# Layer 0 aggregation of a GAT kernel: the weighted rows go to fourteen places of their own, and a gather waits for the multiplication that read its place instead of for the sums

## The chip, the cores and the metric

One Trainium2 chip, one of its cores. The metric is the device time of one execution in microseconds (us). The kernel before was run three times, with a median of 2488.86 us.

## What is computed

A graph attention network of two layers, followed by a mixture-of-experts feed-forward part, on 3125 nodes with 768 features and 50000 edges sorted by destination. The part that matters here is the first layer's message passing, with 8 heads of 96 features:

```python
h = (x @ W1).reshape(n, 8, 96)
e = leaky_relu(al_s[src] + al_d[dst], 0.2)
ex = exp(e - segment_max(e, dst)[dst])
alpha = ex / (segment_sum(ex, dst)[dst] + 1e-16)
out = segment_sum(h[src] * alpha[:, :, None], dst)      # per edge: fetch a row, weight it by head, add it to its node
```

The second layer is the same with one head, and the experts come after it.

## The kernel before

**Stages.** One program calls a row of functions one after the other: the set-up, the features h of all nodes (written to a table `feat_tab` in memory), the attention scores, `aggregate` (this is the changed one), the next layer's features, its scores, `aggregate_rows`, the routing and the experts. Each function is a block with one hand-written instruction stream for each engine, and the streams meet by semaphores alone. On one engine the instructions run in the order in which they are written.

**The work of `aggregate`.** The edges are cut into NT = 392 tiles of 128 edges. For each tile:

1. POOL (GpSimd, L1449) issues one indirect DMA, called a gather here, that fetches 128 rows of 776 floats from `feat_tab` (768 features and 8 columns for the denominator), 397 KB in all, into one of RING = UN = 14 places. Place k = t mod 14 of tile t is `rows[k]`: places 0 to 6 lie in the buffer `ring`, 7 to 10 in `work`, 11 in `wg`, 12 and 13 in `edges`. So a trace row tells by its buffer which places it is about.
2. DVE (VectorE, L1479) multiplies the row by its 8 edge weights, which lie in PSUM (`ex_ps`), **in place**: it reads `rows[k]` and writes `rows[k]`.
3. PE (TensorE, L1502) adds the tile to the sums of a window of 64 destination nodes in PSUM: two matmuls with the tile's 128x64 one-hot matrix, one for each half of 388 columns. The profile shows four matmul records for these two. Where a window of 64 nodes ends inside a tile, the next window is opened by two more matmuls (`opened`, 49 in all).

Beside this, DVE builds the one-hot matrices for 7 tiles at a time (`hots`, L1462) and copies 14 tiles' weights to PSUM (`weights`, L1470). ACT (ScalarE) copies each finished window out of PSUM (L1582, two instructions), prepares the one-hot matrix of the next opening (L1570) and stores the sums of 128 nodes at a time (L1587).

**What orders the work.** The loop of DVE, per turn i of 14 tiles and half j: `hots(i, j)`, in the second half `weights(i + 1)`, then seven multiplications. The waits are:

- the gather of tile t (from t = 14 on) waits until PE has finished the sums of tile t - 13: `tile_mm >= t - UN + 2`, at L1448;
- the multiplication waits for its gather's data (`row_in[k]`), L1477;
- PE's sums wait for the multiplication (`msg_ready`) and, at each seventh tile, for the one-hot matrices (`hot_ready`), L1510 and L1511;
- `hots(i, j)` waits until PE has started the previous batch of seven (`batch_mm >= i * 2 + j`), L1461, since two batches of one-hot matrices are kept;
- ACT's copy of a window waits until PE has opened the next (`open_mm`), L1580, and an opening waits until ACT has emptied the bank (`flushed`).

`big` is a large buffer that holds features in other stages. Nothing in this stage uses it.

Of the kernel before, what the change touches and what calls it, by code (L numbers as in the profile page):

```python
# [4 lines left out]
P = 128  # L5
# [7 lines left out]
UN = 14  # L13
# [34 lines left out]
ROW = 776  # L48
HALF = ROW // 2
HC = ROW // 8  # L50
# [57 lines left out]
def gnn_ffn(nc, io, out):  # L108
    with ExitStack() as ctx:
# [34 lines left out]
        big = sb("big", [P, KC * NP])  # L144
# [1282 lines left out]
        def aggregate():  # L1427
            H = HEADS[0]
            L = "_a0"
            row_in = [sem(f"row_in{k}" + L) for k in range(RING)]  # L1430
            msg_ready, hot_ready, open_ready, tile_mm, open_mm, table_ready = (
                sem(n + L) for n in ("msg", "hot_ready", "open_hot", "tile_mm", "open_mm", "open_table"))
# [3 lines left out]
            ex_ps = [mps[:, h, 0:UN * H].rearrange("p (t h) -> p t h", h=H) for h in range(2)]  # L1436
            iota_ps = tps[:, 1, 0:WIN]
            rows = msg_rows + [edges[:, j * ROW:(j + 1) * ROW] for j in range(RING - len(msg_rows))]
            hot_x = hot_open.rearrange("p (b n) -> p b n", b=NW)

            with nc.Block() as block:
                @block.gpsimd
                def _(pool):
                    nc.gpsimd.memset(zeros, 0.0).then_inc(zero_set, 1)
                    for t in range(NT):
                        k = t % UN
                        if t >= UN:
                            pool.wait_ge(tile_mm, t - UN + 2)  # L1448
                        pool.indirect_dma_start(rows[k], None, feat_tab[0],  # L1449
                                                bass.IndirectOffsetOnAxis(ap=src_t[:, t:t + 1], axis=0)).then_inc(row_in[k], 16)  # L1450

                @block.vector
                def _(dve):
                    V = nc.vector
                    near = iota_ps.unsqueeze(1)

                    def hots(i, j):

                        first = i * UN + j * BATCH
                        if i > 0:  # L1460
                            dve.wait_ge(batch_mm, i * 2 + j)  # L1461
                        V.tensor_tensor(onehot[:, j * BATCH:(j + 1) * BATCH, :], near.to_broadcast([P, BATCH, WIN]),  # L1462
                                        dst_rel[:, first:first + BATCH].unsqueeze(2).to_broadcast([P, BATCH, WIN]),
                                        ALU.is_equal).then_inc(hot_ready, 1)

                    def weights(i):

                        if i >= 2:
                            dve.wait_ge(msg_ready, (i - 1) * UN)
                        V.tensor_copy(ex_ps[i % 2], ex[:, i * UN:(i + 1) * UN, :]).then_inc(ex_set, 1)  # L1470

                    def messages(i, j):

                        if j == 0:
                            dve.wait_ge(ex_set, i + 2)
                        for k in range(j * BATCH, (j + 1) * BATCH):
                            dve.wait_ge(row_in[k], i * 16 + 16)  # L1477
                            r3 = rows[k].rearrange("p (h c) -> p h c", h=H)
                            V.tensor_tensor(r3, r3, ex_ps[i % 2][:, k, :].unsqueeze(2).to_broadcast([P, H, HC]),  # L1479
                                            ALU.mult).then_inc(msg_ready, 1)  # L1480
                    V.tensor_copy(iota_ps, iota_f[:, 0:WIN]).then_inc(ex_set, 1)
                    dve.wait_ge(ex_set, 1)
                    hots(0, 0)
                    hots(0, 1)
                    weights(0)
                    V.tensor_tensor(hot_x, near.to_broadcast([P, NW, WIN]),
                                    dst_open[:, :].unsqueeze(2).to_broadcast([P, NW, WIN]), ALU.is_equal).then_inc(table_ready, 1)
                    for i in range(TURNS):
                        for j in range(2):
                            if i > 0:  # L1490
                                hots(i, j)
                            if j == 1 and i < TURNS - 1:
                                weights(i + 1)
                            messages(i, j)

                @block.tensor
                def _(pe):
                    def sums(hot, k, bank, start):

                        row = rows[k]  # L1500
                        for c in range(WPB):
                            m = nc.tensor.matmul(acc[c * WIN:(c + 1) * WIN, bank, 0:HALF], hot, row[:, c * HALF:(c + 1) * HALF],  # L1502
                                                 start=start, stop=True, skip_group_check=True)
                            if c == 0 and not start and k % BATCH == 0:
                                m.then_inc(batch_mm, 1)
                        return m

                    def added(i, k, bank):
                        if k % BATCH == 0:
                            pe.wait_ge(hot_ready, i * 2 + (k // BATCH + 1))  # L1510
                        pe.wait_ge(msg_ready, i * UN + (k + 1))  # L1511
                        sums(onehot[:, k, :], k, bank, False).then_inc(tile_mm, 1)

                    def opened(b, k, bank):
                        pe.wait_ge(open_ready, b)
                        pe.wait_ge(flushed, b)
                        sums(next_x[bank], k, bank, True).then_inc(open_mm, 1)
                    pe.wait_ge(zero_set, 1)
                    for c in range(WPB):
                        m = nc.tensor.matmul(acc[c * WIN:(c + 1) * WIN, 0, 0:HALF], zeros[:, 0:WIN], zeros[:, 0:HALF], start=True, stop=True,  # L1520
                                             skip_group_check=True)
                    m.then_inc(open_mm, 1)
                    bits_reg = [pe.alloc_register("bits0")]
                    regs = [pe.alloc_register(f"open0_{j}") for j in range(3)]
                    bank_reg = pe.alloc_register("bank0")
                    pe.reg_mov(bank_reg, 0)

                    def single(i, k, b0, b1):
                        bank = pe.snap(bank_reg, min_val=0, max_val=1)
                        with pe.If(bank > 0):  # L1530
                            added(i, k, 1)
                        with pe.Else():
                            added(i, k, 0)
                        with pe.If(b1 > b0):
                            with pe.Fori(b0 + 1, b1 + 1) as b:
                                pe.reg_mov(bank_reg, b & 1)
                                bank = pe.snap(bank_reg, min_val=0, max_val=1)
                                with pe.If(bank > 0):
                                    opened(b, k, 1)
                                with pe.Else():  # L1540
                                    opened(b, k, 0)

                    with pe.Fori(0, TURNS) as i:
                        pe.load(bits_reg, open_bits[0:1, ds(i, 1)])
                        bits = pe.snap(bits_reg[0], min_val=0, max_val=(1 << UN) - 1)
                        for k in range(0, UN, 2):
                            with pe.If((bits & (3 << k)) > 0):
                                pe.load(regs, pair_ends[0:1, ds(i * (UN * 4) + k * 4, 3)])
                                b0, b1, b2 = [pe.snap(r, min_val=0, max_val=NW - 1) for r in regs]
                                single(i, k, b0, b1)  # L1550
                                single(i, k + 1, b1, b2)
                            with pe.Else():
                                bank = pe.snap(bank_reg, min_val=0, max_val=1)
                                with pe.If(bank > 0):
                                    added(i, k, 1)
                                    added(i, k + 1, 1)
                                with pe.Else():
                                    added(i, k, 0)
                                    added(i, k + 1, 0)
                    nc.tensor.matmul(tps[0:32, 0, 0:1], iota_f[:, 0:32], iota_f[:, 0:1], start=True, stop=True,  # L1560
                                     skip_group_check=True).then_inc(open_mm, 1)
# [756 lines left out]
```

## Time and profile before

| | us |
|---|---|
| runs of the kernel before | 2483.84, 2488.86, 2489.7 (median 2488.86) |
| the profiled execution, its own time | 2504.38 |
| its span in the profile | 2502.5 |
| mean granted clock of TensorE | 0.899 of full |
| the stage from the first gather of L1449 to the end of its last copy | about 529 to 1111 |

One execution was profiled; every duration below comes from it. A time in a timeline row is counted from the start of the span. The "idle before" of a row is the time its engine did nothing just ahead of it, with what the profile takes to have ended that. Where an instruction waits for several things, or the named one is long done, the profile's releaser isn't the real one; the text says so where that matters. A row with xN joins N instructions that ran on without a gap.

### The profile page before, as it was taken

Reading aid. Unit: us, or ns where it says so; the run is one execution under the profiler, and the core shown is the slowest. Engines: PE = TensorE matmul, PEld = TensorE weight load, DVE = VectorE, ACT = ScalarE, POOL = GpSimd, SP = SyncE. Lnnn points to the kernel's source line nnn. Section 1 sums busy time; section 2 is a strip of 40 time slices with the busy share of each in tenths; the row PEclk is TensorE's granted clock in tenths of the full one; section 3 lists DMA queues with packets and bytes.
Section 4 is the critical chain, followed back from the end, with each engine's and each line's share of the span. In section 5 each row is a group of like instructions: output and inputs, shape, how many; then the busy total and the mean of one; then the engine's idle time right before and its main releaser. Section 6 shows DMA issues by size and latency. Waiting matters only on the chain. (4 is left out here: it accounts for less than half of the span.)

```text
span 2502.5 us, 32295 instructions
## 1 busy us (share of the span) xinstructions
PE 1881.4 (75%) x8856; PEld 1001.4 (40%) x8857; DVE 1312.2 (52%) x2900; ACT 715.7 (29%) x1721; POOL 1263.7 (50%) x1279
## 2 busy tenths in 40 slices
PE   1837887957777777756789867778777775899997
PEld 1325555522222222224445433333323323677775
DVE  7626667847676667658467412344343447522221
ACT  1514433211001101017223233443444440133332
POOL 5065553036666666632321135666666660277775
PEclk9968998979988999988889978888999996799999
DMA  5322321168888888889589597898998986388886
GB/s 177 114 59 56 100 62 43 54 201 288 289 285 291 287 285 292 281 274 277 154 220 265 124 295 268 314 319 305 316 311 310 323 306 235 84 139 139 138 138 104
DMA packets 171459, 533.04 MB, mean 213 GB/s; under 512 B 35105, under 2 KB 66060, under 8 KB 171122
## 3 DMA queue, kind: packets, MB, share of 16 engines
q0 software_dynamic: 99088, 379.24, 53.5%
q1 hardware_dynamic: 61490, 123.21, 14.1%
q10 hardware_dynamic: 10800, 29.70, 3.0%
q8 instruction: 28, 0.46, 0.1%
q14 instruction: 53, 0.43, 0.0%
HBM read 444.94 MB, written 87.10 MB: 213 GB/s over the span
## 5 line engine op out<-in xcount | busy, mean ns | idle before, releaser
L1502 PE MATMUL acc<-ring,work 128*64 128x388 f32 x880 | 208.2, 556 | 85.2 <-issue 61.3
L1796 PE MATMUL acc<-ring,work 128*64 128x384 f32 (+1 forms) x880 | 203.6, 570 | 80.4 <-issue 72.1
L920 PE MATMUL acc<-wg,work 128*128 128x384 f32 x600 | 224.7, 517 | 26.9 <-issue 17.7
L1640 POOL DMA_INDIRECT ring<-feat_tab,src_t x196 | 187.3, 955 | 109.4 <-PE acc L1796 46.6
L1907 ACT ACTIVATE work<-big,edges 128x64 f32<-128x64 f32 x392 | 135.9, 427 | 352.0 <-DMA edges<-in_w_slow 190.3
L1449 POOL DMA_INDIRECT ring<-feat_tab,src_t x196 | 185.3, 945 | 98.1 <-issue 47.6
L1253 PE MATMUL acc<-wg,work 128*128 128x384 f32 x600 | 217.8, 511 | 8.1 <-issue 6.3
L2109 POOL DMA_INDIRECT out_rows<-ring,wg x114 | 178.0, 1562 | 81.2 <-ACT ring L2206 60.0
L1754 DVE COPY work<-acc 64x384 f32<-64x384 f32 x100 | 56.0, 560 | 308.3 <-DMA edges<-in_w_scale 261.6
L1479 DVE TENSOR_TENSOR ring<-ring,mps 128x776 f32<-128x776 f32 x196 | 183.5, 959 | 56.9 <-DMA ring<-feat_tab,src_t 48.1
L869 POOL DMA_INDIRECT edges<-score_tab,src_p x152 | 147.4, 970 | 116.1 <-issue 45.2
L1582 ACT ACTIVATE work<-acc 64x388 f32<-64x388 f32 x100 | 48.8, 488 | 518.2 <-DMA edges<-in_a_dst 492.2
L1502 PE MATMUL acc<-work 128*64 128x388 f32 x504 | 124.4, 552 | 51.6 <-issue 40.7
L1502 PEld LDWEIGHTS acc<-ring,work 128*64 128x64 f32 x880 | 65.4, 148 | 227.1 <-issue 171.6
L1796 PEld LDWEIGHTS acc<-ring,work 128*64 128x64 f32 x880 | 71.7, 153 | 203.3 <-issue 196.0
L920 PEld LDWEIGHTS acc<-wg,work 128*128 128x128 f32 x600 | 114.2, 201 | 96.5 <-issue 41.4
L2243 DVE TENSOR_TENSOR edges<-acc,wg 128x192 f32<-128x192 f32 x57 | 20.4, 358 | 240.6 <-issue 124.7
L1253 PEld LDWEIGHTS acc<-wg,work 128*128 128x128 f32 x600 | 113.6, 197 | 78.1 <-issue 14.6
L1796 PE MATMUL acc<-work 128*64 128x384 f32 (+1 forms) x504 | 111.8, 519 | 41.9 <-issue 38.3
L1640 POOL DMA_INDIRECT work<-feat_tab,src_t x112 | 106.6, 952 | 60.8 <-issue 27.8
L1449 POOL DMA_INDIRECT work<-feat_tab,src_t x112 | 105.8, 945 | 61.3 <-issue 25.0
L2143 PE MATMUL acc<-big,work 128*128 x684 | 123.6, 331 | 12.3 <-issue 11.4
(388 smaller groups left out, 3498.4 us busy)
## 6 DMA issues: line engine op xcount, KB each, us to landing
ring<-lo_rows SPq DMA_DIRECT2D x49, 256.0 KB
edges<-in_w_slow SPq DMA_DIRECT2D x28, 384.0 KB, 6.0
edges<-in_w_hebb POOLq DMA_DIRECT2D x28, 384.0 KB, 7.2
edges<-in_w_fast POOLq DMA_DIRECT2D x28, 384.0 KB, 8.6
unit_sum<-edges SPq DMA_DIRECT2D x28, 384.0 KB, 5.9
out_rows<-work SPq DMA_DIRECT2D x52, 192.0 KB
feat_tab<-work ACTq DMA_DIRECT2D x25, 388.0 KB
agg_raw<-work ACTq DMA_DIRECT2D x25, 388.0 KB
```

Of the source, the lines that this page charges most:

```text
L869: pool.indirect_dma_start(src_s[:, t, :], None, score_tab, bass.IndirectOffsetOnAxis(ap=src_p[:, t:t + 1], axis=0)).then_inc(gather_in, 16)
L920: m = nc.tensor.matmul(acc[:, sl * 2 + c, 0:C // 2], xT[sl][:, k, :], wg[:, k, c * (C // 2):(c + 1) * (C // 2)], start=(k == 0), stop=(k = ...
L1253: m = nc.tensor.matmul(acc[:, sl * 2 + c, 0:C // 2], xT[sl][:, k, :], wg[:, k, c * (C // 2):(c + 1) * (C // 2)], start=(k == 0), stop=(k = ...
L1449: pool.indirect_dma_start(rows[k], None, feat_tab[0], bass.IndirectOffsetOnAxis(ap=src_t[:, t:t + 1], axis=0)).then_inc(row_in[k], 16)
L1479: V.tensor_tensor(r3, r3, ex_ps[i % 2][:, k, :].unsqueeze(2).to_broadcast([P, H, HC]), ALU.mult).then_inc(msg_ready, 1)
L1502: m = nc.tensor.matmul(acc[c * WIN:(c + 1) * WIN, bank, 0:HALF], hot, row[:, c * HALF:(c + 1) * HALF], start=start, stop=True, skip_group_ ...
L1640: pool.indirect_dma_start(rows[k][:, 0:C], None, feat_tab[1], bass.IndirectOffsetOnAxis(ap=src_t[:, t:t + 1], axis=0)).then_inc(row_in[k], 16)
L1754: ins = V.tensor_copy(r[w * WIN:(w + 1) * WIN, c * CHUNK:c * CHUNK + n], acc[c * WIN:(c + 1) * WIN, q % 2, 0:n])
L1796: m = nc.tensor.matmul(acc[c * WIN:(c + 1) * WIN, bank, 0:n], hot, row[:, c * CHUNK:c * CHUNK + n], start=start, stop=True, skip_group_che ...
L1907: ins = nc.scalar.activation(onehot[:, j * BATCH + k, :], gaps[j][:, k, :], ACT.Relu, bias=ex[:, first + k:first + k + 1], scale=neg_ex[:, ...
L2109: pool.indirect_dma_start(out[c], bass.IndirectOffsetOnAxis(ap=slots[:, 2, t:t + 1].bitcast(i32), axis=0), y_rows[t % TU][:, c * (C // 2): ...
L2143: m = nc.tensor.matmul(acc[:, 2, 0:HID], xTs[k][:, c, :], big[:, ds(e * HID + c * EH, HID)], start=(c == 0), stop=(c == KC - 1))
```

## The change

The products get a place of their own: `msgs[k]` is the k-th piece, one row long, of `big`, for k = 0 to 13. The multiplication reads `rows[k]` and writes `msgs[k]`, and PE reads `msgs[k]`. With this the waits change:

- the gather of tile t waits until DVE has multiplied tile t - 14 (`msg_ready >= t - 13`), not until PE has summed tile t - 13;
- the multiplication of tile t (from t = 14 on) waits also until PE has summed tile t - 13 (`tile_mm >= t - 12`), after its wait for the data.

No instruction is added, removed or moved on any engine: POOL, DVE and PE have as many as before, in the same order. The lines move: the gather stands at L1450 and PE's sums at L1505 in the changed kernel.

```diff
@@ -1436,6 +1436,7 @@
             rows = msg_rows + [edges[:, j * ROW:(j + 1) * ROW] for j in range(RING - len(msg_rows))]
+            msgs = [big[:, k * ROW:(k + 1) * ROW] for k in range(UN)]
             hot_x = hot_open.rearrange("p (b n) -> p b n", b=NW)
@@ -1445,7 +1446,7 @@
                     for t in range(NT):
                         k = t % UN
                         if t >= UN:
-                            pool.wait_ge(tile_mm, t - UN + 2)
+                            pool.wait_ge(msg_ready, t - UN + 1)
                         pool.indirect_dma_start(rows[k], None, feat_tab[0],
@@ -1475,8 +1476,10 @@
                             dve.wait_ge(row_in[k], i * 16 + 16)
-                            r3 = rows[k].rearrange("p (h c) -> p h c", h=H)
-                            V.tensor_tensor(r3, r3, ex_ps[i % 2][:, k, :].unsqueeze(2).to_broadcast([P, H, HC]),
+                            if i > 0:
+                                dve.wait_ge(tile_mm, (i - 1) * UN + k + 2)
+                            m3, r3 = (of[k].rearrange("p (h c) -> p h c", h=H) for of in (msgs, rows))
+                            V.tensor_tensor(m3, r3, ex_ps[i % 2][:, k, :].unsqueeze(2).to_broadcast([P, H, HC]),
                                             ALU.mult).then_inc(msg_ready, 1)
@@ -1497,7 +1500,7 @@
                     def sums(hot, k, bank, start):
-                        row = rows[k]
+                        row = msgs[k]
```

## Rows read from the trace of the kernel before

**Rows 1.** Busy us (and count) by engine, TensorE clock, DMA share, GB/s, of the stage.
```profile
527.00:1112.00 585.00, 419.60 (x1770) 129.74 (x1770) 404.32 (x478) 58.73 (x150) 370.91 (x393) 0.92 0.85 283
```

**Rows 2.** The gathers of L1449: durations, first and last start, idle before them.
```profile
L1449 POOL DMA_INDIRECT ring<-feat_tab,src_t x196: 940/946/955, 529.1 to 1091.5; - x196
...
L1449 POOL DMA_INDIRECT edges<-feat_tab,src_t x56: 940/946/955, 544.1 to 1102.0; - x56
...
  issue: 91.4, 297
  DMA score_tab<-al_node: 70.2, 44
  PE acc L1502: 42.0, 51
```

**Rows 3.** Timeline of POOL at the stage's start: start, duration, instruction, idle before it.
```profile
550.36 0.95 POOL L1449 DMA_INDIRECT ring<-feat_tab,src_t  x1 [0.30 <-issue]
551.62 0.95 POOL L1449 DMA_INDIRECT ring<-feat_tab,src_t  x1 [0.30 <-issue]
555.73 0.94 POOL L1449 DMA_INDIRECT ring<-feat_tab,src_t  x1 [3.17 <-DMA score_tab<-al_node]
```

**Rows 4.** Timeline of PE, DVE and ACT in the same stretch.
```profile
543.96 0.87 PE L1502 MATMUL acc<-ring,work 128*64 128x388 f32 x4 [0.54 <-issue]
...
544.66 0.83 PE L1502 MATMUL acc<-work 128*64 128x388 f32 x4
...
554.13 1.56 PE L1502 MATMUL acc<-work 128*64 128x388 f32 x4 [5.58 <-issue]
...
555.54 0.62 DVE L1462 TENSOR_TENSOR work<-tps,dst_rel 128x448 f32<-128x448 f32 x1 [3.86 <-DMA keep<-in_dst_last]
```

**Rows 5.** Waits of the stage, by who waited: us, times, longest.
```profile
PEld acc L1502 <- issue: 345.3, 522, 6.3
...
DVE work L1462 <- DMA keep<-in_dst_last: 72.4, 38, 4.0
```

**Rows 6.** Timeline of the stage's end, after the last gather.
```profile
1102.04 0.94 POOL L1449 DMA_INDIRECT edges<-feat_tab,src_t  x1 [0.30 <-issue]
...
1106.60 2.50 PE L1502 MATMUL acc<-edges,work 128*64 128x388 f32 x12 [1.28 <-DVE edges L1479]
...
1108.37 2.00 ACT L1582 ACTIVATE work<-acc 64x388 f32<-64x388 f32 x4 [3.43 <-PE acc L1502]
```

**Rows 7.** Timeline of an earlier stage (scores), where gathers run beside PE too.
```profile
234.78 1.21 PE L908 MATMUL tps<-edges,ring 128*128 128x200 bf16 x12
...
241.84 1.06 DVE L1058 TENSOR_TENSOR edges<-tps,edges 128x400 f32<-128x400 f32 x2 [4.35 <-remote]
242.12 0.94 POOL L869 DMA_INDIRECT edges<-score_tab,src_p  x1 [2.20 <-remote]
```

**Rows 8.** The multiplications of L1479: durations in ns, idle before them.
```profile
L1479 DVE TENSOR_TENSOR ring<-ring,mps x196: 950/961/965, 533.8 to 1096.2; 128x776 f32<-128x776 f32 x196
...
  DMA ring<-feat_tab,src_t: 48.1, 68
```

**Rows 9.** DMA queues of the stage: share of 16 engines in the last column.
```profile
q0 software_dynamic: 31360, 155.77, 81.2%
q10 hardware_dynamic: 3580, 9.87, 4.2%
```

**Rows 10.** As rows 1, for the stretch in which no gather had paused yet.
```profile
534.00:554.00 20.00, 11.95 (x44) 3.56 (x44) 13.47 (x15) 0.00 (x0) 14.19 (x15) 0.76 0.94 324
```

**Rows 11.** The build of seven tiles' one-hot matrices, L1462.
```profile
L1462 DVE TENSOR_TENSOR work<-tps,dst_rel x56: 611/624/626, 528.3 to 1099.4; 128x448 f32<-128x448 f32 x56
```

**Rows 12.** The gathers of the second aggregation, L1640, in which DVE multiplies no rows.
```profile
L1640 POOL DMA_INDIRECT ring<-feat_tab,src_t x196: 940/946/1212, 1480.9 to 2059.2; - x196
...
L1640 POOL DMA_INDIRECT edges<-feat_tab,src_t x56: 942/946/1209, 1496.3 to 2069.8; - x56
...
  PE acc L1796: 88.1, 69
```

**Rows 13.** Timeline of the experts: a POOL transfer that waits for ACT.
```profile
2207.20 0.81 ACT L2206 ACTIVATE ring<-acc 128x768 f32<-128x768 f32 x1 [1.78 <-PE acc L2159]
...
2208.29 1.57 POOL L2109 DMA_INDIRECT out_rows<-ring,wg  x1 [0.68 <-ACT ring L2206]
```

## The prediction

> **What bounds the kernel now.** The windows view comes first, to see what the stage is worth: 585 us, in which DVE is busy 404 us, POOL 371 and the DMA engines 85%, so none of them is full [rows 1]. PE's 420 us are of little use as a measure, since its records sit beside many waits. Next, the group of the gathers, because every tile begins with one: 392 of them from 529.1 to 1102.0, so 572.9 / 391 = **1.465 us for each tile** [rows 2]. The third view is POOL's timeline. A gather takes 0.95 us, and after it POOL idles 0.30 us even where nothing holds it, so 1.25 us is what POOL alone would need [rows 3]. The first 19 gathers run at just that. What lies over it is in the idle times of the group: those put down to a DMA and to PE are 70.2 + 42.0 us in 95 gathers; less 0.30 us each, which is always there, that is 112.2 - 28.5 = **84 us of pauses** [rows 2]. This agrees with 572.9 - 391 x 1.25 = 84. The DMA `score_tab<-al_node` was done long before; the only thing a gather waits for here is PE's count of summed tiles.
>
> So is PE too slow? The timelines of PE and DVE answer this. The twentieth gather (t = 19) needs the sums of tile 6, the last tile of a turn that lies in `ring`. PE's four records on it end at 543.96 + 0.87 = 544.83 [rows 4], yet the gather starts at 555.73, 11 us later, after 3.17 us of idle time [rows 3]. `hots(1, 0)` needs the start of tile 7, the first in `work`: its records end at 545.49, and DVE, idle for 3.86 us, begins at 555.54 [rows 4]. Meanwhile PE itself stands still for 5.58 us until 554.13 with multiplied rows before it [rows 4]; over the stage the weight loads wait 345 us in 522 places for nothing that the profile can name [rows 5]. So **PE's work is early and its counts reach the others late**, in bunches, and after a standstill of POOL: gather, `hots` and PE all go on within 2 us.
>
> When are they prompt? At the stage's end, once no gather is left to wait: PE's last matmuls start at 1106.60, and ACT goes on with the window at 1108.37, while they still run [rows 6]. In the stage of the scores, gathers wait for PE as well; there DVE's reading of the matmul that ended at 235.99 starts at 241.84, again just as POOL comes back from a pause, at 242.12 [rows 7]. My reading is that a gather which is queued on POOL with its wait for PE's count unfulfilled, behind gathers that run, holds up PE's reports. The records don't show that mechanism, only that the two go together.
>
> **The change part by part.**
>
> *The gather's wait.* It now asks for the multiplication of tile t - 14. By the first tile, whose gather starts at 529.1 and whose multiplication ends at 533.8 + 0.96 = 534.8 [rows 2, 8], that is 5.7 us after its gather; the gather of tile t follows 14 x 1.25 = 17.5 us after that of t - 14. So the wait is fulfilled 11.8 us early, and the pauses of 84 us have nothing left to end them. This is the upper end of the gain. The other end is nothing, or less (rivals).
>
> *What is late next.* First DMA: the gathers take 81.2% and the stores 4.2% of 585 us [rows 9], 499.6 us of all 16 engines. The fullest long stretch is that without pauses, at 0.94 and 324 GB/s [rows 10]. At 0.94 the stage needs 499.6 / 0.94 = 531.5 us, a gain of 53. Between 84 (POOL's issue is the limit) and 53 (DMA never gets fuller than the row shows) I take the middle, **68 us**, since 1.25 us for each gather was held in that very stretch, but without stores beside it. The tile then takes (572.9 - 68) / 391 = 1.29 us.
>
> *DVE's new wait, 392 times.* No instruction is added, so the wait alone counts. It stands behind the wait for the data. It asks for tile t - 13, which was multiplied 13 x 1.29 = 16.8 us earlier, and PE needs about 0.87 us after that; so it costs nothing even if the count came 11 us late as in rows 3. Cover left: some 5 us. Behind it in DVE's order stand the other multiplications and, each seventh tile, `hots`. `hots` is the tighter wait: PE must have begun the batch before, whose first tile was multiplied 6 x 1.29 = 7.7 us before its last; less 0.87 us for that tile's matmuls, a count that comes under 6.9 us late is free there; the 72.4 us of DVE's idle time [rows 5] go with prompt counts.
>
> *DVE's work.* Seven multiplications of 0.961, one build of 0.624 and half a copy of weights, below 0.2, make 7.55 us of the 9.03 that seven tiles take at 1.29: 84% [rows 8, 11]. Writing to another place instead of back is not in the trace; it has the same elements and types, the same PSUM operand, so I cost it at nothing. For it to matter, a multiplication would have to grow from 0.96 to (9.03 - 0.8) / 7 = 1.18 us. Its other bound is no gain, as DVE isn't the limit.
>
> *PE's work.* It reads another address: nothing. 441 pairs of matmuls (392 tiles and 49 openings) at 0.87 us for four records [rows 4] are 384 us, under the 505 that are left.
>
> *Sum.* The gain is 68 us of the profiled execution's 2504.4, which gives 2436. That execution was 15.5 us over the median of the three runs; I take the gain from the median: 2488.9 - 68 = **2421 us**.
>
> **The rivals.**
>
> *A: the reports are late by themselves (no change).* If the lateness comes with the gathers or with PE's own stream, and not with a gather that waits for PE, `hots` keeps the pace: seven tiles at today's 1.465 are 10.25 us, and the build (0.62), a multiplication (0.96), the tile's matmuls (0.87) and a count that is 7.8 us late fill them. The gathers then wait for a multiplication that waits for `hots`. The stage stays: 2489, or down to 2482 where a little slack is won. For it: the second aggregation, where DVE multiplies nothing, has the same pace, (2069.8 - 1480.9) / 391 = 1.506, and 88 us of waits for PE [rows 12], though this pace has the same wait of gathers for PE. Against it: the prompt hand-overs of rows 6, and of the stage's first 12 us.
>
> *B: the lateness moves to DVE's count (slower).* The gathers now wait for DVE. If a queued gather holds up whatever engine it waits for, then DVE's count of products is late, and that one PE needs for every tile, not one in seven. It decides once the wait is still open when the gather is queued, that is when data and multiplication come later after their gather than now, which fuller DMA queues make likely. Price: the pause of rows 3, 3.17 - 0.30 = 2.87 us, in each of 392 / 9 = 44 bunches is 126 us in place of 84: 42 us slower, **2531**. Against it: in the experts a POOL transfer waits for ACT's count, and starts 2208.29 - 2208.01 = 0.28 us after ACT's end [rows 13]. In the trace only PE's counts are late.
>
> The Trainium skill (TensorE: Matmul & The Clock Gate, section "Architectural detail: the array is 16× 32×32, not 1× 128×128") gives TensorE a queue of 64 instructions and GpSimd one of 8, in strict order. By this page a gather would be queued up to 8 ahead, and the 11.8 us shrink to an estimated 11.8 - 8 x 1.25 = 1.8 us, so that B would begin with a landing 2 us later than at the start. By rows alone the slack is the full 11.8 us; no row shows the depth of a queue.
>
> *C: DMA is the limit and gets no fuller than the stage's mean of 0.85 to 0.90.* The second half of the gain is lost: 499.6 / 0.90 = 555, a gain of 30, 2459. It is on the forecast's side.
>
> **How the numbers follow.** A measurement of this kernel can tell about 0.3% from no change, 7.5 us. Forecast (gain 53 to 84, 2405 to 2436) 0.50; C 0.14, so faster is 0.64. A has 0.17, all of it in "same". B has 0.19, with prices from just over 0.3% to 2531. The range leaves out the worse half of B and gains over 89 us: from 2400 to 2500. The likeliest case's own range is 2405 to 2436.
>
> **What would show it.** Right: POOL's idle time before gathers falls to 0.30 us nearly throughout, about 39 gathers in 50 us instead of 34; the wait of `hots` falls from 72 us to under 15; ACT's copies follow the openings at once; the DMA share of the stage rises from 0.85 to above 0.92; the stage is about 517 us. A would show the same 1.46 us for each tile, the gathers' waits now put down to DVE, and `hots` still waiting 60 us or more. B would show PE idle on DVE's products that were ready long before, and multiplications that come late after landed data. The prediction is wrong in its root if PE's counts still reach `hots` late with no gather waiting for them. It is wrong only in size if they are prompt and the tile takes other than 1.25 to 1.36 us.

## The result, and the profile after

The changed kernel is **slower: 2547.9 us** (median of 4 runs) against 2489.3 for the kernel before, ratio 1.0239, 95% interval 1.0213 to 1.0265. The forecast was 2421. (The median of the kernel before is that of four runs here, with one of 2492.79 more than above.) Below, the stage in the windows view of the changed kernel (columns as in [rows 1]):

```profile
522.00:1158.00 636.00, 383.54 (x1770) 133.76 (x1770) 385.14 (x478) 57.83 (x149) 370.96 (x393) 0.80 0.76 260
```

It answers to [rows 1]: every engine runs the same number of its counted instructions (ACT's 149 and 150 differ at the window's edge), and POOL is busy for 371 us both times. But the DMA share is 0.76 instead of 0.85, and TensorE's mean granted clock is 0.80 instead of 0.92, in a stage in which its weight loads stand idle for 445.8 us without a named reason, instead of 345.3. The group of the gathers answers to [rows 2]:

```profile
L1450 POOL DMA_INDIRECT ring<-feat_tab,src_t x196: 942/946/955, 524.1 to 1126.1; - x196
...
L1450 POOL DMA_INDIRECT edges<-feat_tab,src_t x56: 942/946/955, 539.1 to 1140.0; - x56
...
  DVE big L1482: 159.4, 106
  issue: 87.1, 286
```

From first gather to last it is 1140.0 - 524.1 = 615.9 us, before 572.9: **1.575 us for each tile instead of 1.465**, 43 us in all. Another 10 come after the last gather: the last copy of a window ends 19 us after it, before 8 us. Together that is 54 of the 59 us by which the medians differ. The gathers wait for nothing but DVE now, as intended, and for 159 us; without the 0.30 us behind every gather the pauses are 615.9 - 391 x 1.25 = 127 us, before 84. POOL's timeline shows how:

```profile
566.66 0.95 POOL L1450 DMA_INDIRECT ring<-feat_tab,src_t  x1 [0.30 <-issue]
575.02 0.94 POOL L1450 DMA_INDIRECT work<-feat_tab,src_t  x1 [7.41 <-DVE big L1482]
...
643.40 0.94 POOL L1450 DMA_INDIRECT work<-feat_tab,src_t  x1 [5.37 <-DVE big L1482]
665.38 0.94 POOL L1450 DMA_INDIRECT work<-feat_tab,src_t  x1 [4.78 <-DVE big L1482]
...
687.33 0.94 POOL L1450 DMA_INDIRECT work<-feat_tab,src_t  x1 [4.80 <-DVE big L1482]
```

The first 35 gathers run without a pause, 1.25 us each, which the prediction had hoped for throughout. Then POOL stops for 7.4 us, and from there the stage is a regular beat: **14 gathers, a stop of 4.8 us** (26 stops in all, of 4.7 to 7.4 us, with a median of 4.8). Without the usual 0.30 that is (14 x 1.25 + 4.5) / 14 = 1.571 us for each tile. The waits of the stage say who waits for what:

```profile
PEld acc L1505 <- issue: 445.8, 622, 14.4
...
POOL work L1450 <- DVE big L1482: 142.9, 52, 7.4
DVE work L1463 <- DMA keep<-in_dst_last: 126.5, 16, 8.5
DVE work L1463 <- PE acc L1505: 111.8, 19, 16.7
```

These answer to [rows 5]. DVE is idle for 126.5 + 111.8 = 238 us before its builds of one-hot matrices, in place of 72. Its multiplications hardly wait for data any more. So the chain is: gather waits for multiplication, multiplication for the build, the build for PE's count. (The `DMA keep<-in_dst_last` that is named was done long before; the build's wait is for PE.) One stop, on all engines but the weight loads:

```profile
679.49 2.85 PE L1505 MATMUL acc<-big,work 128*64 128x388 f32 x8 [4.70 <-issue]
...
681.59 0.95 POOL L1450 DMA_INDIRECT ring<-feat_tab,src_t  x1 [0.30 <-issue]
685.11 0.98 ACT L1585 ACTIVATE work<-acc 64x388 f32<-64x388 f32 x2 [20.32 <-DMA edges<-in_a_dst]
685.39 0.62 DVE L1463 TENSOR_TENSOR work<-tps,dst_rel 128x448 f32<-128x448 f32 x1 [8.40 <-DMA keep<-in_dst_last]
685.45 6.92 PE L1505 MATMUL acc<-big,work 128*64 128x388 f32 x32 [3.10 <-issue]
...
686.11 3.57 DVE L1482 TENSOR_TENSOR big<-work,mps 128x776 f32<-128x776 f32 x4
...
687.33 0.94 POOL L1450 DMA_INDIRECT work<-feat_tab,src_t  x1 [4.80 <-DVE big L1482]
```

The last gather of the bunch ends at 682.54. Only then, at 685.1 to 685.5, ACT (idle for 20 us), DVE (8.4 us) and PE go on together. POOL gets its own release later still: the build takes 0.62 us, the multiplication 0.95, and the gather starts at 687.33. In the kernel before, the gather itself waited for the count and went on with the others.

**Is the count late, or PE itself?** The trace also keeps when a semaphore was raised, and PE's own register and branch instructions (its stream is a loop with branches around the matmuls), which the profile doesn't count as busy. Both say more than the rows above. In the kernel before, PE had done the matmul that a waiting build asks for in every case; all of DVE's idle time there is a count that came late, by 4 to 10 us. In the changed kernel it isn't so: of DVE's 238 us, **144 pass before PE has done that matmul** and 95 after it (144 and 96 in a second trace, f1; a matmul's end is modelled, so these are rough). In the stop above PE does it from 679.49 to 681.04, after a pause of 4.7 us, and the count is raised at 685.37. PE's lateness goes with a slow stream of its own. One group of its register instructions, by the view of its line, first in the changed kernel and then in g4 of experiment 2, in which POOL issues no gather (the three durations are the shortest, the median and the longest in ns):

```profile
L1550 PEldq ALU_OP  x196: 3/36/715, 524.9 to 1153.4; - x196
```

```profile
L1553 PEldq ALU_OP  x196: 36/36/36, 526.6 to 939.2; - x196
```

From the first gather to the last, 142 of 1214 such instructions (`ALU_OP`, `MOVE`, `FUSED_REGOPS`) take over 0.5 us, most of them 0.70; before it is 20 of 1251. They don't stand just anywhere: none of the 631 that begin in the first six gathers of a bunch is slow, but 119 of the 297 in the later ones are. The counts go late a little sooner. Of those of matmuls that end within the first four gathers of a bunch, 134 of 181 are raised within 0.1 us; of the later ones 6 of 236. In the kernel before, where POOL goes on as soon as its count has come, hardly any is prompt: 17 of 281 and 7 of 185. (Some records of counts are missing, so these are lower bounds.)

### The profile page after: what moved, and what is told of

Same layout as the page of the kernel before. It is cut to its first block and busy times, and to the rows that moved or that the text cites. A ratio compares the mean times of both kernels' runs of the same rounds, so it can differ in the third digit from the quotient of the medians.

```text
span 2543.1 us, 32646 instructions
## 1 busy us (share of the span) xinstructions
PE 1831.2 (72%) x8856; PEld 1002.3 (39%) x8857; DVE 1293.2 (51%) x2900; ACT 715.2 (28%) x1721; POOL 1265.0 (50%) x1279
## 5 line engine op out<-in xcount | busy, mean ns | idle before, releaser
L1505 PE MATMUL acc<-big,work 128*64 128x388 f32 x1764 | 382.5, 580 | 250.4 <-issue 235.4
L1505 PEld LDWEIGHTS acc<-big,work 128*64 128x64 f32 x1764 | 133.4, 157 | 499.5 <-issue 445.8
L1799 PE MATMUL acc<-ring,work 128*64 128x384 f32 (+1 forms) x880 | 197.1, 547 | 87.4 <-issue 79.4
L1450 POOL DMA_INDIRECT ring<-feat_tab,src_t x196 | 185.3, 945 | 59.8 <-issue 55.1
L1450 POOL DMA_INDIRECT work<-feat_tab,src_t x112 | 105.8, 945 | 161.1 <-DVE big L1482 142.9
L1482 DVE TENSOR_TENSOR big<-ring,mps 128x776 f32<-128x776 f32 x196 | 173.9, 956 | 2.3 <-DMA ring<-feat_tab,src_t 1.9
L1463 DVE TENSOR_TENSOR work<-tps,dst_rel 128x448 f32<-128x448 f32 x56 | 34.8, 623 | 239.1 <-DMA keep<-in_dst_last 126.5
L1799 PEld LDWEIGHTS acc<-ring,work 128*64 128x64 f32 x880 | 70.5, 147 | 205.8 <-issue 198.6
```

The source lines that it names most:

```text
L1450: pool.indirect_dma_start(rows[k], None, feat_tab[0], bass.IndirectOffsetOnAxis(ap=src_t[:, t:t + 1], axis=0)).then_inc(row_in[k], 16)
L1482: V.tensor_tensor(m3, r3, ex_ps[i % 2][:, k, :].unsqueeze(2).to_broadcast([P, H, HC]), ALU.mult).then_inc(msg_ready, 1)
L1799: m = nc.tensor.matmul(acc[c * WIN:(c + 1) * WIN, bank, 0:n], hot, row[:, c * CHUNK:c * CHUNK + n], start=start, stop=True, skip_group_che ...
```

## The experiments

A result is given as its ratio to the kernel before on the same chip, with its 95% interval. The chips differ: the kernel before took 2246 us on the chip of the first four runs (e), and 2490 to 2506 on the three of the others; one of these three gave 2490 for the runs f and 2506 later for the runs i, so only numbers taken side by side are compared. On the first, PE's counts are never late: in all four of its traces all 56 counts of a batch (the ones that the builds wait for) are raised within 0.02 us of the matmul's end. In a trace of the kernel before on another chip (f2) it is 6.5 us in the median.

**1. Is it the places, the run-ahead, or the DMA traffic?** First, the places alone (the wait of the gathers is set back):

```diff
-                            pool.wait_ge(msg_ready, t - UN + 1)
+                            pool.wait_ge(tile_mm, t - UN + 2)
```

> The changed kernel, but the gathers wait for PE's sums again; the products still go to their own places and DVE keeps its wait. Theory P (PE's counts come through only when POOL stops issuing gathers; a gather's wait for PE made POOL stop early, after 7 to 9 gathers, so it paced the stage): the time is that of before, 2480 to 2497, pauses of about 2 us every 7 to 9 gathers. Rival W (writing to another buffer or DVE's additional wait costs the time): 2530 to 2550 as in the changed kernel.

Measured: 2243.6 us, 0.9995 (0.9984 to 1.0007), on the chip with prompt counts. The same kernel on a chip with late counts:

> Own places for the products, but the gathers wait for PE's sums as before. Theory P on a chip with late counts: as the kernel before, within 0.5%, since a gather's wait for PE stops POOL early. Rival W (the places and DVE's wait cost the time): 2% slower there. On a chip with prompt counts all expect no change.

Measured: 2490.8, **1.0008** (0.9997 to 1.0020). Writing elsewhere, and DVE's 378 additional waits (the first turn of 14 has none), cost nothing; rival W has fallen. The waits are instructions after all, about 0.02 us each: the profile of the changed kernel has 32646 instructions, before 32295. In this run they are never open, since the gather has waited for the same sums; in the changed kernel hardly ever, as the multiplications are idle for 5 us there in all. On the first chip the profile of this kernel shows what the prediction took for the outcome of the change:

```profile
L1450 POOL DMA_INDIRECT ring<-feat_tab,src_t x196: 942/946/958, 455.7 to 935.8; - x196
...
L1450 POOL DMA_INDIRECT edges<-feat_tab,src_t x56: 942/946/955, 470.8 to 944.5; - x56
...
  issue: 82.8, 272
  PE acc L1505: 36.6, 120
```

(944.5 - 455.7) / 391 = 1.25 us for each tile: all idle time is the 0.30 us behind each gather, though these gathers wait for PE. Its stage has a DMA share of 0.93:

```profile
454.00:955.00 501.00, 364.19 (x1770) 111.00 (x1770) 403.94 (x478) 58.57 (x149) 371.07 (x393) 0.95 0.93 330
```

Then the data. From the fifteenth tile on, a gather fetches 97 floats in place of 776 (and from other rows, so the sums are wrong):

```diff
+                        part = (rows[k], feat_tab[0]) if t < UN else (rows[k][:, 0:HC], feat_tab[0].rearrange("r (x c) -> (r x) c", x=8))
-                        pool.indirect_dma_start(rows[k], None, feat_tab[0],
+                        pool.indirect_dma_start(part[0], None, part[1],
```

> The changed kernel, but from the fifteenth tile on a gather fetches 97 of the 776 floats of each row, so most of the data is left out; POOL issues as many gathers as before. Theory P (POOL's issuing of gathers holds up PE's counts): little changes, bunches of 14 gathers and pauses near 4.8 us stay, 1.5 us or more for each tile. Rival D (the gathers' data, the nearly full DMA engines, hold them up): PE's counts come at once, DVE's build of one-hot matrices hardly waits, and a tile takes 1.25 to 1.3 us, so that the kernel takes about 2420.

> The changed kernel with an eighth of each row fetched from the fifteenth tile on; the rest of the data is left out. On a chip with late counts, theory P (POOL's issuing holds up PE's counts): as slow as the changed kernel, 2520 or more. Rival D (full DMA engines hold them up): about 2420, DVE's builds hardly wait. On a chip with prompt counts no theory expects anything but 2240.

Measured: 2239.2 on the chip with prompt counts (one run, it tells nothing apart there) and 2545.2 on one with late counts (one run), beside these two, on the latter:

> The changed kernel as it is. The chip of the last four runs ran the kernel before in 2246 instead of 2489, and PE's counts came without delay in all four. Theory Q (the time that the change costs hangs on late PE counts, which some chips have in this program and some don't): where the kernel before takes about 2246, this one takes 2236 to 2250, no change; where it takes about 2489, this one takes 2535 to 2560. Rival R (the change costs time by its waits or places wherever it runs): slower than before by 1.5% or more in both.

> The kernel before as it is, for its profile on this chip. Theory Q: at about 2246 the gathers run at 1.25 us each without pauses and DVE never waits for PE before it builds one-hot matrices; at about 2489 the pauses of 2 us are there. Rival R expects pauses of gathers in both, smaller ones at 2246.

The changed kernel took 2548.1, 1.0232 (1.0215 to 1.0249), the kernel before 2492.6. The small rows are as slow as the whole ones with the DMA engines at a fifth, and with the same stops:

```profile
527.00:1140.00 613.00, 363.64 (x1670) 127.40 (x1670) 369.77 (x459) 54.60 (x140) 367.62 (x389) 0.78 0.20 54
```

```profile
668.92 0.94 POOL L1451 DMA_INDIRECT work<-feat_tab,src_t  x1 [4.77 <-DVE big L1483]
690.93 0.95 POOL L1451 DMA_INDIRECT work<-feat_tab,src_t  x1 [4.82 <-DVE big L1483]
```

So the traffic (D) isn't it. Of theory Q, that chips differ is shown for the kernel before and for three variants; the changed kernel as it is was not run on the chip with prompt counts. The nearest to it there is e4 of experiment 5, which costs nothing either.

**2. Rows fetched without POOL.** SyncE issues the fetches, blocks of 128 rows in place of the edges' rows (so the sums are of other rows):

```diff
+                @block.sync
+                def _(sp):
...
+                            sp.wait_ge(msg_ready, t - UN + 1)
+                        b = t % NB
+                        sp.dma_start(rows[k], feat_tab[0][b * P:(b + 1) * P, :]).then_inc(row_in[k], 16)
```

> The changed kernel, but SyncE issues the fetches with plain DMAs of 128 rows in a block, same size, same waits; POOL issues none. The rows are not those of the edges. Theory P: PE's counts come at once (waits of L1463 on PE below 20 us in all), and a tile takes what DMA or DVE needs, 1.1 to 1.35 us. Rival D: the counts stay late, with idle times of DVE before the one-hot build of 100 us or more, as long as the DMA share is above 0.9.

> The changed kernel with the fetches issued by SyncE as plain DMAs of blocks of 128 rows (not the edges' rows), POOL issues none. Theory P on a chip with late counts: they come at once, DVE's idle time before the builds falls from over 200 us to under 20, and the stage takes 1.0 to 1.15 us for each tile as on the chip of the first run (441 us for the stage there). Rival D: the counts stay late, since the DMA engines are fuller than ever.

Measured: 2163.5 and, with late counts in the kernel before beside it (2489.7), **2328.1** (one run each). There the DMA engines are full, and DVE's builds wait for nothing (first the windows view of 100 us, then the row of the builds: busy, mean ns, idle before):

```profile
600.00:700.00 100.00, 81.97 (x434) 28.27 (x432) 95.40 (x118) 14.12 (x36) 0.00 (x0) 0.98 1.03 405
```

```profile
L1466 DVE TENSOR_TENSOR work<-tps,dst_rel 128x448 f32<-128x448 f32 x56 | 34.5, 618 | 0.0
```

With the same waits, and no gather on POOL, PE's counts are prompt, at 1.06 us for each tile. The stage now takes the same time on both chips: from the first build to the last 409 us in each run (456.6 to 865.6 and 525.0 to 934.1). Without gathers, nothing is left of the difference between the chips here; the 165 us between the two runs lie in the other stages. Is it gathers, or any work of POOL? POOL now writes 128x900 zeros for each tile beside this:

> SyncE fetches blocks of rows as in the run with rows by SyncE (2328 where before takes 2490), and POOL writes 128x900 zeros for each tile to an unused piece, about 0.95 us each, with the gathers' waits. If any busy POOL holds up PE's counts: bunches, DVE idle before its builds for 100 us or more, 2450 or more. If only gathers do: 2320 to 2350.

Measured: 2341.9 beside 2502.0, and again no wait before the builds:

```profile
L1452 POOL MEMSET big<- 128x900 f32 x392 | 329.9, 847 | 72.6 <-DVE big L1492 55.6
...
L1473 DVE TENSOR_TENSOR work<-tps,dst_rel 128x448 f32<-128x448 f32 x56 | 34.5, 618 | 0.0
```

A POOL that is 330 us busy with memsets doesn't delay the counts. Gathers do. Whether it is POOL's work on a gather or the kind of DMA that it issues isn't told apart: SyncE's fetches also go through another queue (`q1 hardware_dynamic`, not `q0 software_dynamic`). The number of DMA packets isn't it: 56382 in that queue here, and no delay; 13088 in the other with the small rows, and the full delay.

**3. Queued gathers, or running ones?** POOL's sequencer is held back by a branch that waits for the landing of five gathers back:

```diff
+                        if t >= 5:
+                            pool.wait_ge(row_in[(t - 5) % UN], 16 * ((t - 5) // UN + 1))
+                            with pool.If(bits > 16382):
+                                pool.sem_inc(seen, 1)
```

> The changed kernel, but before each gather from the sixth on POOL's sequencer takes a branch that waits until the rows of the gather five back have landed, so that hardly more than one gather is queued ahead of POOL's work, while POOL itself should not pause (landing takes 4.3 to 4.7 us, five gathers 6.25). Theory S (PE's counts are held up because gathers stand queued far ahead on POOL): the counts come at once, 1.25 to 1.32 us for each tile, 2405 to 2440 where before takes 2490. Theory G (the running gathers themselves hold them up, however few are queued): bunches and stops as in the changed kernel, 2530 to 2560.

Measured: 2555.4, 1.0216 (1.0177 to 1.0255). The trace shows the branch of a gather run when the gather ahead of it is about to start, so hardly more than one is queued. Late counts and stops stay, and the time; the beat gets irregular. Its 40 stops, of 0.7 to 8.5 us, come after 1 to 23 gathers and add up to 120 us of pauses (127 in the changed kernel). Two of the regular ones:

```profile
732.77 0.94 POOL L1458 DMA_INDIRECT work<-feat_tab,src_t  x1 [4.64 <-DVE big L1490]
754.80 0.94 POOL L1458 DMA_INDIRECT work<-feat_tab,src_t  x1 [4.82 <-DVE big L1490]
```

(754.80 - 732.77 = 22.0 us for 14 gathers.) Theory S has fallen. The prediction's own theory, a queued gather whose wait for PE is open, had fallen before: in the changed kernel no gather waits for PE, and the counts are late.

**4. Fewer reports.** PE no longer counts each tile; the count at each batch's first tile, which `hots` waits for anyway, frees the places. In the kernel before, the gathers wait for that count (`batch_mm >= t // BATCH`).

```diff
-                            if i > 0:
-                                dve.wait_ge(tile_mm, (i - 1) * UN + k + 2)
...
-                        sums(onehot[:, k, :], k, bank, False).then_inc(tile_mm, 1)
+                        sums(onehot[:, k, :], k, bank, False)
```

> The changed kernel, but PE no longer counts each tile (392 reports less): the count at each batch's first tile, which the builds of one-hot matrices wait for anyway, covers the places of the products, and DVE's wait of its own is dropped. Theory P2 (while POOL streams gathers, a report of PE takes some 5 us to get through, so the number of reports is what costs): with 105 instead of 497 reports the stage keeps up, 1.25 to 1.35 us for each tile, 2400 to 2440 on a chip where the kernel before takes 2490. Theory P1 (no report gets through until POOL stops, however few there are): 2530 or more. On a chip where the kernel before takes 2246: no change in either.

> The kernel before (products in place), with the same edit: PE counts at each batch's first tile alone, and a gather waits for that count, so POOL runs 7 to 13 tiles ahead of PE instead of 13. Theory P2: 2420 to 2460 where before takes 2490; part of the gain is lost to the coarser wait. Theory P1: 2480 to 2510. Where before takes 2246: 2246 to 2275, since only the coarser wait is left.

Measured: 2537.7, 1.0187 (1.0154 to 1.0221), and 2522.5, 1.0126 (1.0095 to 1.0157). A fifth of the reports takes some 11 us off the changed kernel by the ratios (1.0187, and 1.0232 on another chip), not the 100 and more that P2 asked for; P2 has fallen. The second was a miss of P1 too (2480 to 2510): its gathers run in bunches of 14 or 7, with stops of 1.0 to 6.2 us, so here it is the coarser wait that lengthens the bunches.

**5. How long a bunch, how long a stop?** Gathers at most eight tiles ahead of the multiplications (`msg_ready >= t - 7`):

> The changed kernel, but a gather waits for the multiplication eight tiles back instead of fourteen, so POOL can run at most eight tiles ahead of DVE. Theory P: POOL stops earlier after DVE has stopped for its one-hot matrices, the bunches are shorter, and the time falls back towards that of before, 2480 to 2515. Rival D says the same if shorter bunches empty the DMA queues sooner. Rival W: no gain against the changed kernel, 2540 or more.

> The changed kernel with gathers at most eight tiles ahead of the multiplications. Theory P on a chip with late counts: POOL stops sooner after DVE has stopped, so bunches are shorter and the time falls back from 2548 to 2480 to 2515. If it stays at 2540 or more, stopping POOL is not what lets the counts through. On a chip with prompt counts: 2243 as in the first run of it.

Measured: 2243.4, 0.9995 (0.9983 to 1.0007), on the first chip; 2542.3, 1.0210 (1.0176 to 1.0245), with late counts, where 2480 to 2515 was expected. By the words on record, 2540 or more meant that stopping POOL is not what lets the counts through. The trace shows that the edit didn't test this: it stops in bunches of 14 all the same, at other places, for 4.3 to 6.2 us nearly every time. DVE does two batches once a count has come, and then waits for the next. As long as gathers wait for DVE, their bunch is set by DVE's two batches. The test is that of the last two runs below.

Now a second wait on the changed kernel's gathers, for PE's sums of tile t - 15:

```diff
                             pool.wait_ge(msg_ready, t - UN + 1)
+                        if t >= 15:
+                            pool.wait_ge(tile_mm, t - 14)
```

> The changed kernel with a second wait on each gather from t = 15 on: PE has summed tile t - 15 (its own place allows two tiles more than before's t - 13). Theory P (POOL has to stop for the counts; waiting for the count itself ends the stop as soon as it arrives, waiting for the multiplication ends it only after build and multiplication): stops of 2 us as in before, after bunches of 8 to 10 gathers, 2465 to 2495, although only a wait is added to a kernel of 2548. Rival W: 2548 or more.

Measured: 2515.8, 1.0065 (1.0043 to 1.0087), over the range expected (2465 to 2495). **A wait more on each gather takes about 40 us off the changed kernel** (by the ratios, 1.0065 and 1.0232, on two chips). Its bunches are mostly of 9 to 12 gathers, its stops mostly of 2.6 to 3.2 us, and its waits for the multiplication have fallen from 159 to 26 us:

```profile
  issue: 84.7, 272
  DMA score_tab<-al_node: 60.0, 25
  PE acc L1507: 44.0, 49
  DVE big L1484: 25.5, 46
```

The other way, the kernel before with the sums of tile t - 11 (`tile_mm >= t - 10` from t = 12 on):

> The kernel before, but a gather waits for the sums of tile t - 11 instead of t - 13, so POOL stops two gathers earlier. Theory G (a run of gathers holds up PE's counts until POOL stops for about 2 us): if the length of a stop is fixed, shorter bunches cost time, 2500 to 2530; if it shrinks with the bunch, no change, 2480 to 2498, where before takes 2490.

Measured: 2505.7, 0.9999 (0.9988 to 1.0011). Stops after seven or eight gathers as before; DVE's idle time before the builds falls from 72 to 12 us and buys nothing, so that wait was cover for POOL's stops, not a cost of its own.

Last, stops of a set kind in the changed kernel:

```diff
+                        if t % 5 == 4:
+                            pool.wait_ge(row_in[(t - 3) % UN], 16 * ((t - 3) // UN + 1))
```

and the same with every fourth gather (`t % 4 == 3`).

> The changed kernel, but every fifth gather also waits until the rows of the gather three back have landed, which at 4.3 to 4.7 us for a landing stops POOL for about 1 us. After a stop the counts were prompt for some four gathers. If 1 us lets them through, DVE hardly waits before its builds and a tile takes (6.25 + 0.8) / 5 = 1.41 us, 2465 to 2480 where before takes 2490. If 1 us is too short: late counts and stops as in the changed kernel on top of it, 2545 or more.

> As the one before, with every fourth gather: (5.0 + 0.8) / 4 = 1.45 us, 2480 to 2492 if 1 us is enough; if it isn't after five gathers but is after four, this one alone is faster than the changed kernel; if it isn't at all, 2545 or more.

Measured: 2547.2, 1.0170 (1.0146 to 1.0193), and 2598.1, 1.0365 (1.0327 to 1.0403). Both miss their ranges for prompt counts (2465 to 2480 and 2480 to 2492), and the times by themselves would have stood for late ones. The traces say otherwise. The stops came out twice as long as reckoned, and the builds (same row in both runs) wait for nothing:

```profile
636.87 0.95 POOL L1452 DMA_INDIRECT edges<-feat_tab,src_t  x1 [1.84 <-issue]
644.58 0.95 POOL L1452 DMA_INDIRECT ring<-feat_tab,src_t  x1 [1.75 <-issue]
```

```profile
L1465 DVE TENSOR_TENSOR work<-tps,dst_rel 128x448 f32<-128x448 f32 x56 | 34.5, 618 | 0.0
```

With 1.8 us after every fifth gather DVE never waits for a count again: such a stop is enough. Every count of a batch that the two traces recorded (46 and 48 of 56) is raised within 0.05 us of a matmul that raises it, and none of PE's 1253 register instructions of i2 is slow. But (6.25 + 1.5) / 5 = 1.55 us for each tile is as dear as the disease (measured 1.571; 1.704 with every fourth). Whether 1 us would do was not reached, and whether it is the stop or the run of only five gathers that keeps the counts prompt isn't told apart; both stay open. No version of mine that fetches the right rows beats the kernel before where counts are late.

**Not tested.** PE's stream in this stage is a loop with branches, and it is its register and branch instructions that get slow. No run has a PE stream without them, so how much of the loss would stay with straight code isn't known.

## Why the prediction was wrong

**Right.** POOL's pauses were 84 us, and in the kernel before PE's work is early while its counts come late, in bunches, with a standstill of POOL [rows 3, 4]. Own places, DVE's wait (378 times, not 392) and PE's new address cost nothing (experiment 1). DVE's multiplications stayed at 0.96 us.

**The step that failed** is "the pauses of 84 us have nothing left to end them". It took the pauses for the price of a gather's open wait for PE. They were what let PE's counts through: a long run of gathers holds the counts back whatever the gathers wait for (PE in the kernel before and f3, DVE in f1, f4, g1 and h1). The counts come only after POOL has stopped, after 1.9 us in the median in the kernel before (the gather then goes on), and after 2.9 us in the changed one (the build goes on). In place of no pauses there were 127 us of them. I had seen that counts came "after a standstill of POOL", and read the standstill as a consequence only. The evidence for my reading, prompt counts at the stage's end [rows 6], fits the other just as well, since there no gather runs either. It was the weakest place of the argument, and no row told the two apart. The prediction had named this itself as being "wrong in its root": counts that reach `hots` late with no gather waiting for them; DVE's idle time there went from 72 to 238 us.

With that step went the cover of 11.8 us. It was read off the first tile, multiplied 5.7 us after its gather. The gather of tile 91 starts at 665.38 in the changed kernel, and its multiplication ends at 687.1, 21.7 us later: 4 us too late for the gather of tile 105, which would have been due after 17.5.

**What happened in its place.** With the old wait POOL stops by itself after some eight gathers and goes on at the moment the count arrives: (8 x 1.25 + 1.6) / 8 = 1.45 us. With the new one it streams 14. From about the fifth gather on the counts are late, from the seventh PE's own stream is slow too and PE falls behind, and POOL's release comes only after count, build and multiplication: 4.8 us (2.9 until the build, 1.9 from there), 1.57. The 0.11 us between 1.465 and 1.575, 391 times, are the 43 us measured between the gathers, and 10 more come at the end. None of the terms for DMA or for POOL's issue was ever reached. The chip with prompt counts shows that POOL's was sized well, 1.25 us, but DMA's wasn't: the stage of e1 takes 501 us at a share of 0.93, which is 466 us of all 16 engines and not 499.6, so at 0.94 DMA alone would need 496 us and not 531.5. By its time of 2246 us the kernel before is at that pace on this chip already.

**Rival B** had the right sign and the wrong mechanism: DVE's counts are prompt (the multiplication ends at 687.1, the gather behind it starts at 687.33), as the row of the experts had suggested with ACT's count [rows 13]. That its pauses of 126 us in place of 84 nearly meet the measured 127 is luck: it had 44 stops of 2.87 us, and there are 26 of 4.9, with another cause. The Trainium skill (TensorE: Matmul & The Clock Gate, section "Architectural detail: the array is 16× 32×32, not 1× 128×128") gives GpSimd's queue as eight deep. Held to about one gather ahead, the kernel took the same time (h1, 1.0216 against 1.0232), so the depth decides nothing here.

**Rival A** had the mechanism and the wrong price. It said that the lateness comes "with the gathers or with PE's own stream", that gathers would wait for a multiplication that waits for `hots`, and this is the chain above. SyncE's fetches rule out PE's stream by itself (prompt at 1.06 us for each tile), and leave the gathers. Its price was no change, since it kept the count 7.8 us late and PE's work on time. The count is up to 9.9 us late for a build, and PE itself is late besides, which makes up 144 of the 238 us.

**The range** left this out because it priced the unknown by the pauses alone, both ways. The row that would have bounded it was in view: DVE idle for 3.9 us and PE for 5.6 in one stop [rows 4]. If POOL was to wait for DVE behind that, each stop had to grow, by a build and a multiplication at least.

## What to carry to other kernels

Before a wait is moved away from a slow signal, ask whether the wait is also what lets the signal come. If an idle stretch of one engine coincides with the arrival of another's counts, test the direction: let a third engine do the work (here SyncE's fetches) and see whether the counts are still late. And if a stall cannot be avoided, let the engine wait for the late count itself and not for work that stands two steps behind it. Where an engine is idle for "issue", look at its register and branch instructions (`--source` of their lines) before you call only its counts late.

## What was unexpected of the hardware

- While POOL runs gathers one after the other (0.95 us each, one every 1.25), the others see PE's counts late: 6.5 us in the median for a build's count in the kernel before (f2), 12.9 us for the one that ACT waits for in the stop shown above (PE did the matmul by 672.2, the count was raised at 685.08). DVE's counts, and PE's beside memsets on POOL, aren't affected.
- PE's own register instructions go from 0.04 to 0.70 us each then, in the changed kernel from the seventh gather of a bunch on, and PE stands still between its matmuls. A bunch of five with a stop of 1.8 us shows neither. What inside the chip does this no run shows.
- It depends on the chip: none of it on the chip of the first four runs, all of it on three others. The whole kernel takes 2246 us there and 2490 to 2506 on the others, a tenth of the time; the stage with SyncE's fetches takes 409 us on both kinds.
- The number of reports (497 or 105) and the data behind the gathers (all or an eighth) make no difference to it beyond some 11 us.
